# POOL copies the gather's indices itself, the target logits are picked four slots at a time ahead of the waits for rows, and the logits reach the buckets by small matmuls

## The reference

```python
h = (x_flat @ W_gat).reshape(M, HEADS, NUM_EXPERTS)
a_src = (h * att_src).sum(-1)
a_dst = (h * att_dst).sum(-1)
e = leaky_relu(a_src[src] + a_dst[dst], 0.2)
ee = exp(e - segment_max(e, dst)[dst])
alpha = ee / (segment_sum(ee, dst)[dst] + 1e-16)
msg = h[src] * alpha[:, :, None]
agg = segment_sum(msg, dst) + b_gat
scores = layernorm(agg, gamma, beta).mean over heads
# per token: the best 2 of 4 experts, softmax of their scores, gated sum of the experts' outputs
```

## Time and profile before

| what | value |
|---|---|
| median of three runs | 1071.6 us (1069.84 to 1073.52) |
| the profiled execution | 1072.75 us, span 1071.0 us |
| mean granted TensorE clock | 0.869 |
| busy: PE, DVE, ACT, POOL | 793.4, 668.0, 355.3, 180.1 us |
| gathers (L592) | 88 of 1085 ns in the mean, from 825.8 to 975.3 us |

### The profile page before, as it was taken

One profiled execution on the slowest core, in us unless ns is written; L12 is line 12 of the kernel. 1 busy time (PEld: TensorE's weight loads), 2 busy tenths in 40 slices (PEclk: granted clock), 3 DMA queues, 4 the chain that ended last, 5 costly groups with the idle time before them and its releaser, 6 DMA issues.

```text
span 1071.0 us, 15105 instructions
## 1 busy us (share of the span) xinstructions
PE 793.4 (74%) x4837; PEld 519.7 (49%) x4837; DVE 668.0 (62%) x1393; ACT 355.3 (33%) x552; POOL 180.1 (17%) x179
## 2 busy tenths in 40 slices
PE   4369920017999989989988788799759877662688
PEld 1212220016887878878853233444327555442477
DVE  3599778755656656646648777595664434435764
ACT  3421130004544544545542333430022443333451
POOL 5180010000000000000022000100001366773021
PEclk9589965557999999999999899999977988886599
DMA  8000000001000000000000000000012200010001
GB/s 310 0 1 1 1 0 0 2 39 42 2 1 0 0 0 0 0 0 0 0 0 1 0 0 0 2 1 0 2 42 16 8 7 7 7 6 4 3 21 59
DMA packets 15645, 15.63 MB, mean 15 GB/s; under 512 B 9664, under 2 KB 13376, under 8 KB 15216
## 3 DMA queue, kind: packets, MB, share of 16 engines
q1 hardware_dynamic: 12544, 14.00, 4.3%
q0 software_dynamic: 3056, 1.08, 1.7%
HBM read 10.42 MB, written 4.65 MB: 14 GB/s over the span
## 4 chain that ended last, share of the span: by engine, by line
PE 19%; DVE 16%; issue 12%; POOL 3%; DMA 2%; DVEq 2%; ACT 2%; POOLq 0%; PEldq 0%; PEld 0%; SPq 0%; ACTq 0%
PE banks L1557 17%; DVE kept L1229 2%; POOL rows_g L592 2%; DMA rows_g<-table_d,g_idx 2%; DVE wide_buf L1189 1%; DVE wide_buf L1195 1%; PE banks L1838 1%; DVE tie L1193 1%; DVE kept L1292 1%; DVE kept L1386 1%; DVE T L867 1%; DVE round_k L1291 1%; PE banks L1590 1%; DVE shared L1384 1%; ACT wide_buf L776 1%
## 5 line engine op out<-in xcount | busy, mean ns | idle before, releaser
L1138 DVE TENSOR_TENSOR wide_buf<-banks,small 128x1024 f32<-128x1024 f32 x72 | 88.2, 1225 | 117.9 <-ACT small L726 117.9
L1557 PE MATMUL banks<-wide_buf 128*128 128x256 f32 (+1 forms) x720 | 144.6, 349 | 0.0
L1557 PEld LDWEIGHTS banks<-wide_buf 128*128 128x128 f32 x720 | 122.3, 194 | 12.6
L1557 PEld LDWEIGHTS banks<-XP 128*128 128x128 bf16 (+1 forms) x1552 | 101.8, 132 | 47.2 <-DVE XP L992 27.6
L1557 PE MATMUL banks<-XP 128*128 128x32 bf16 (+1 forms) x1552 | 102.4, 213 | 29.5 <-DVE XP L992 27.4
L592 POOL DMA_INDIRECT rows_g<-table_d,g_idx x88 | 95.5, 1085 | 132.2 <-issue 100.4
L1557 PE MATMUL banks<-taps_w,small 128*128 128x128 f32 x618 | 92.2, 296 | 21.0 <-issue 21.0
L1557 PE MATMUL banks<-T,XP 128*128 (+1 forms) x128 | 73.7, 701 | 38.2 <-ACT XP L789 33.3
L1557 PEld LDWEIGHTS banks<-taps_w,small 128*128 128x128 f32 x618 | 85.6, 203 | 31.7 <-issue 22.0
L724 ACT ACTIVATE small<-banks,neg_x 128x512 f32<-128x512 f32 x72 | 49.6, 690 | 150.1 <-PE banks L1557 124.2
L1557 PE MATMUL banks<-shared,sel 128*128 x216 | 60.2, 385 | 32.8 <-DVEq L1131 26.0
(11 more groups left out here) (330 smaller groups left out, 1190.9 us busy)
## 6 DMA issues: line engine op xcount, KB each, us to landing
wide_buf<-in_edges SPq DMA_DIRECT2D x2, 1536.0 KB, 15.4
generic_d<-generic SPq DMA_DIRECT2D x1, 2064.0 KB, 7.3
X<-in_x SPq DMA_DIRECT2D x4, 512.0 KB, 5.3
out_x<-X SPq DMA_DIRECT2D x4, 512.0 KB, 2.6
rows_g<-table_d,g_idx POOLq DMA_INDIRECT x88
wide_buf<-in_edges SPq DMA_DIRECT2D x2, 512.0 KB, 10.0
XP<-in_m_w SPq DMA_DIRECT2D x2, 512.0 KB, 4.7
taps_w<-in_w_dcn SPq DMA_DIRECT2D x1, 576.0 KB, 16.3
```

The source lines that it names most:

```text
L1138: nc.vector.tensor_tensor(near_w[s % RING], banks[:, 0:2, :], hat_x[:, h:h + 1, :].to_broadcast([P, 2, CHUNK]), ALU.mult).then_inc(w_done, 1)
L1557: return nc.tensor.matmul(o, l, r, start=start, stop=stop, **kw)
```

## The change

The indices are no longer copied by DVE: POOL copies four of them in front of each half's gathers and waits for its own copy. DVE's step is two equal halves: first the picks of four slots, then the wait for their rows, then the copy of features and the addition. The target logits no longer pass through DRAM: PE multiplies columns of `a_dst` with slices of the identity (16 matmuls of 128x32 by 128x32), placed in the experts' first iteration, and DVE copies the result. For that a bucket holds another set of 32 nodes: `neg_lo` becomes an input, the layout of `bucket_dst` is head by head, and `slot_sums` takes `q, j = divmod(p, 32)`. `slot_ends` moves ahead of the last node's logits.

```diff
-            sp.wait_ge(adst_ready, 1)
-            sp.dma_start(table_d_dst.rearrange("(t p) h -> p t h", p=P), a_dst[:, :, :]).then_inc(adst_in, 16)
             sp.wait_ge(table_out, 16)
             sp.dma_start(last_row[:, :], table_d[LAST].partition_broadcast(P)).then_inc(last_in, 16)
-            sp.wait_ge(adst_in, 16)
-            sp.dma_start(bucket_dst[:, :, :], table_d_dst.rearrange("(p t) h -> p t h", t=HIS)).then_inc(adst_in, 16)
...
-            def gather(asked, free):
+            def gather(g, r):
                 for half in range(2):
-                    pool.wait_ge(idx1_ready, asked + half + 1)
+                    cols = slice(half * HALF_STEP, (half + 1) * HALF_STEP)
+                    pool.wait_ge(max1_done, g * 2 + half + 1)
                     pool.sem_inc(passed, 1)
-                    pool.wait_ge(max1_done, free + half + 1)
+                    nc.gpsimd.tensor_copy(g_idx[:, cols], slot_idx[:, bass.ds(r * STEP + half * HALF_STEP, HALF_STEP)]).then_inc(idx1_ready, 1)
+                    pool.wait_ge(idx1_ready, g * 2 + half + 1)
                     pool.sem_inc(passed, 1)
...
+                for half in range(2):
+                    cols = bass.ds(r * STEP + half * HALF_STEP, HALF_STEP)
+                    grid = [P, HALF_STEP, HEADS, HIS]
+                    step(nc.vector.tensor_tensor(oh_slots, his[:, cols].unsqueeze(2).to_broadcast([P, HALF_STEP, HIS]),
+                                                 lane[:, 0:HIS].unsqueeze(1).to_broadcast([P, HALF_STEP, HIS]), ALU.is_equal))
+                    step(nc.vector.tensor_tensor(pick_grid, oh_slots.unsqueeze(2).to_broadcast(grid),
+                                                 bucket_dst[:, :, :].unsqueeze(1).to_broadcast(grid), ALU.mult))
+                    step(nc.vector.tensor_reduce(z_by_head[:, :, cols].rearrange("p h k -> p k h"), pick_grid, AX_X, ALU.add))
                     for landed in rows_landed[half]:
                         dve.wait_ge(landed, g * (16 * 2) + 16 * 2)
                         dve.sem_inc(passed, 1)
-                    step(nc.vector.tensor_copy(g_idx[...], slot_idx[...]))
-                    dve.sem_inc(idx1_ready, 1)
-                    step(nc.vector.tensor_copy(feat_s[...], rows_step[...]))
+                    nc.vector.tensor_copy(feat_s[:, :, cols], rows_step[:, half, :, 0:HE].rearrange("p k f -> p f k"))
                     step(nc.vector.tensor_tensor(z_by_head[:, :, cols], z_by_head[:, :, cols], rows_step[...], ALU.add))
                     dve.sem_inc(max1_done, 1)
...
             dve.sem_inc(max1_done, 2)
+            dve.wait_ge(dst_turned, 1)
+            run(nc.vector.tensor_copy(bucket_dst[:, :, :].rearrange("p h t -> p (h t)"), ps[6][:, 0:P]))
+            slot_ends()
             a_src = table[:, :, HE:ROW]
...
-            slot_ends()
-            dve.wait_ge(adst_in, 32)
...
-            with pe.Fori(0, CHUNKS - 1) as i:
+            hidden(0, 0)
+            hidden(0, 1)
+            expert_out(0, 0)
+            pe.wait_ge(adst_ready, 1)
+            for q in range(4):
+                part = slice(q * HIS, (q + 1) * HIS)
+                for h in range(HEADS):
+                    last = mm(ps[6][part, h * HIS:(h + 1) * HIS], a_dst[:, :, h], ident[:, part], True, True)
+            last.then_inc(dst_turned, 1)
+            hidden(0, 2)
+            expert_out(0, 1)
+            hidden(0, 3)
+            expert_out(0, 2)
+            expert_out(0, 3)
+            with pe.Fori(1, CHUNKS - 1) as i:
                 experts(i)
...
                 for p in range(P):
-                    j, q = divmod(p, 4)
+                    q, j = divmod(p, HIS)
```

More of the change, by code:

```diff
@@ L327, in metaformer_kernel @@
         rows_landed = [[rows1_in, sem("rows1_b")], [sem("rows2_in"), sem("rows2_b")]]
-        adst_ready, adst_in, keys_there = (sem(n) for n in ("adst_ready", "adst_in", "keys_there"))
+        adst_ready, dst_turned, keys_there = (sem(n) for n in ("adst_ready", "dst_turned", "keys_there"))
         ends_ready, ends_turned, oh_ready, k_chain, s_chain = (sem(n) for n in (
@@ L466, in _ @@
             pool.dma_start(b_off[0:3 * TAPS, :], a["b_off"].rearrange("(p c) -> p c", c=1)).then_inc(wa_in, 16)
-            for own, name in ((neg_y, "neg_y"), (neg_x, "neg_x"), (y_win, "y_win"), (x_own, "x_own")):
+            for own, name in ((neg_y, "neg_y"), (neg_x, "neg_x"), (neg_lo, "neg_lo"), (y_win, "y_win"), (x_own, "x_own")):
                 pool.dma_start(own[:, :], a[name]).then_inc(wa_in, 16)
@@ L480, in _ @@
                            allow_small_or_imprecise_dtypes=True).then_inc(made2, 1)
-            nc.gpsimd.iota(neg_lo[:, :], [[0, 1]], base=0, channel_multiplier=-(1 << 17),
-                           allow_small_or_imprecise_dtypes=True).then_inc(made2, 1)
+            pool.sem_inc(made2, 1)
             nc.gpsimd.memset(below[:, :, :], 1.0).then_inc(made2, 1)
@@ L593, in gather @@
                                                 bass.IndirectOffsetOnAxis(ap=g_idx[:, c:c + 1], axis=0)).then_inc(rows_landed[half][k // 2], 16)
+            pool.wait_ge(ends_ready, 1)
             with pool.Fori(0, steps) as r:
-                gather(2 * r, 2 * r)
+                gather(r, r)
             with pool.If(rest > 0):
                 with pool.Fori(0, rest) as k:
+                    pool.wait_ge(ends_ready, k + 2)
+                    pool.sem_inc(passed, 1)
                     with pool.Fori(0, STEPS) as r:
-                        gather(k * (2 * STEPS + 2) + (2 * STEPS + 2) + 2 * r, k * (2 * STEPS) + 2 * STEPS + 2 * r)
+                        gather(k * STEPS + STEPS + r, r)
                     pool.nop()
@@ L1325, in _ @@
             norm(ln3, res3, 2)
-            SLOT_KEYS, SLOT_STEP = 13, 3 + 2 * 3
+            SLOT_KEYS, SLOT_STEP = 11, 2 * (3 + 1)
             def slot_keys(R):
@@ L1337, in slot_keys @@
                 step(nc.vector.tensor_tensor(slot_idx[:, 0:P], slot_idx[:, 0:P], slot_lo, ALU.add))
-                for half in range(2):
-                    halves = slice(half * HALF_STEP, (half + 1) * HALF_STEP)
-                    step(nc.vector.tensor_copy(g_idx[:, halves], slot_idx[:, halves]))
-                    dve.sem_inc(idx1_ready, 1)
                 step(nc.vector.tensor_scalar(slot_int, slot_int, 12, None, ALU.arith_shift_right))
@@ L1370, in rows_in @@
                         dve.sem_inc(passed, 1)
-                    step(nc.vector.tensor_copy(g_idx[:, half * HALF_STEP:(half + 1) * HALF_STEP], slot_idx[:, bass.ds(at + STEP, HALF_STEP)]))
-                    dve.sem_inc(idx1_ready, 1)
-                    step(nc.vector.tensor_copy(feat_s[:, :, bass.ds(at, HALF_STEP)], rows_step[:, half, :, 0:HE].rearrange("p k f -> p f k")))
-                def logits_in(half):
-                    cols = bass.ds(r * STEP + half * HALF_STEP, HALF_STEP)
+                    nc.vector.tensor_copy(feat_s[:, :, cols], rows_step[:, half, :, 0:HE].rearrange("p k f -> p f k"))
                     step(nc.vector.tensor_tensor(z_by_head[:, :, cols], z_by_head[:, :, cols],
@@ L1959 @@
               "x_own": f32(np.arange(P)[:, None] % SIDE - 1 + kx), "neg_y": -rows.astype(np.float32),
+              "neg_lo": -f32((np.arange(P) % HIS * 4 + np.arange(P) // HIS)[:, None] * (1 << 17)),
               "neg_x": -(np.arange(P)[:, None] % SIDE).astype(np.float32), "x": np.asarray(inputs["x"])}
```

20 lines of the change are left out of this document (4 added, 16 removed).

## The result

The changed kernel took 1089.5 us (median of 4, 1084.2 to 1099.2) beside 1071.1 of the kernel before: a ratio of 1.0179, 95% interval 1.0103 to 1.0256. It is slower, and outside the range of the forecast. The profiled execution took 1087.37 us, 14.5 more in span than before.

The account below looks back on a forecast made before the run. Two chains side by side, the gathers ending last with only 5.5 us to spare over the experts' loop. 1072.75 - 7.9 - 1.1 + 8.7 = 1072.45 us profiled, 1071.3 on the median's scale, called 1071; 8-in-10 range 1060 to 1083.

Parts of the forecast that it names:

- the pace of the experts' loop: Experts' loop beside gathers keeps 23.95 us an iteration, ending at 974.1; first exponential 7.9 us earlier, not 17.5.
- rival (b): Experts' loop slows as POOL's rest goes: 1079.8 us at 27 us an iteration, 1086 at 30; chance 0.29.
- Rival (a): Experts' loop under gathers runs better than 20 us an iteration, so the gathers set the end: 1061.7 us; chance 0.33.
- The steps: Gather steps: 6.0 us per half, collision included, so ten steps of 12.0 us from 842.3; POOL is the bound.
- The 1.1 us after the first exponential: DVE's product behind the first exponential: its two earlier operations are long done, a gain of 1.1 us.
- the sums: Bucket sums on PE: 256 instructions in one quarter after another at 53.5 ns, 13.7 us against 4.98, +8.7.
- The start: Part before step 1 of the gathers: step 1 begins at 842.3 instead of 850.29, 8.0 us earlier.
- The collision of picks and gathers: Gather steps: two shorter DVE products lie beside gathers in each step, adding 0.15 us per half.
- The 0.69 us a product that I had named as the worst: Gather steps: under an exclusive port lock every product could cost its full 0.69 us, ten steps 10 us longer.
- My +4.5 for a clock that rises halfway: Bucket sums: with PE at 2.4 GHz for the second half, they would cost +4.5 us.
- The 12.8 us: Bucket sums: the skill's some 60 cycles a matmul, at 1.2 GHz, make 12.8 us, +7.8.

Follow-up runs that it names:

- r9: The changed kernel run again without edits on a third chip: 1053.6 us, ratio 0.9847 to the kernel before.
- c15: Changed kernel with bucket sums in the old order, POOL starting a step only when DVE has done both halves of the step before: 1079.3 us (1.0092).
- r10: The kernel before run again without edits on the third chip: 1069.9 us (0.9996).
- c14: Changed kernel with bucket sums in the old order and `bucket_dst` heads innermost, so the picks' multiply is strided: 1057.9 us (0.9870).
- c13: The changed kernel run again without edits on a fourth chip: 1089.0 us, ratio 1.0181 to the kernel before.
- e1: Changed kernel with only the 256 bucket-sum products put back in the old order, round the four column quarters: 1083.0 us (1.0137).

## Why the prediction was wrong

**Failed step: the pace of the experts' loop.** "Kept at that pace", 23.95 us an iteration, was the term; it measured 35.0 in the result and 15.33 in r9. The first put the loop's end at 993.5 where I had 974.1, the second took the loop off the path. The pace was not a constant to be carried over: it depended on how the gathers follow each other, which is what the change alters. I had seen this as rival (b), by the rest on POOL that goes away, which c15 bears out, but stopped its price at 30 us and 1086, and gave it 0.29; the range ended at 1083. The trace of before has a sign of it that I had not put in numbers: seven of its nine held copies start 10.0 to 11.6 us into a step of the gathers, under the stretched eighth gather or in the rest behind it.

**Rival (a), the gathers set the end,** came true in r9, at 1053.6 where I had 1061.7. I had put the holding down to executions being profiled; that is wrong, since the unprofiled runs of the changed kernel took 1084 to 1099 in the one group and 1053 to 1054 in the other. Its sum was off in three terms. The steps: 5.75 us a half (nine steps of r9 take 103.6 us) where I had 6.0, 5 us over 20 halves. The 1.1 us after the first exponential exist only where ACT is late; where the gathers set the end, 14.41 us pass from it to the sums in r9 (959.82 to 974.23), and as many in r10. And the sums.

**The start:** forecast step 1 at 842.3, 8.0 us earlier; 841.62 in the result, and 839.47 against 847.42 in the pair r9 and r10, 7.95. Right. The logits' copy was itself held for 2.1 us in the result (827.71 against 825.56).

**The steps:** POOL's own copy takes 0.20 us, as priced, and the wait behind it 0.79 us, where I had 0.95. The collision of picks and gathers came, but hardly cost anything: POOL's gathers have a mean of 0.96 to 0.97 us with the contiguous multiply. One gather in a step starts under the product, in r9 (timelines of DVE and POOL):
```profile
875.92 0.69 DVE L1366 TENSOR_TENSOR shared<-shared,bucket_dst 128x512 f32<-128x512 f32 x1
...
876.40 1.03 POOL L588 DMA_INDIRECT rows_g<-table_d,g_idx  x1 [0.30 <-issue]
```
It ends 0.82 us behind the product, as the strided pair of c14 above does (0.83), and that of the earlier trace rows (0.82). Only 0.21 us of the short product were left when it started, so it lost 0.08 us. In all traces together, 224 gathers start under such a product so early that their usual 0.94 us would be over less than 0.80 us behind it. Of these 220 end 0.80 to 0.86 us behind it, whether it is strided or not; the other four stand in the last step. A product that starts under a gather keeps its 0.69 us. The Trainium skill (SBUF — State Buffer, section SBUF: two separate sides) calls the shared port pair of DVE and GpSimd an exclusive lock, which a DVE instruction with two SBUF inputs takes only against a GpSimd instruction that reads SBUF. That these gathers behave as if locked out until the product's end agrees with a lock; whether an indirect DMA counts as such a reader, no row tells. The 0.69 us a product that I had named as the worst did not come, since a gather loses only what is left of the product.

**The sums:** 10.61 us, +5.6 instead of +8.7. The price of an instruction was right, and the clock was not: I took the lower one throughout. Stretches of the result's sums, their first third and their last (columns as above), and the whole of c13's:
```profile
1008.49:1012.00 3.51, 3.51 (x69) 3.51 (x70) 1.05 (x1) 0.00 (x0) 0.00 (x0) 0.50 0.00 0
...
1016.00:1019.10 3.10, 3.09 (x101) 2.99 (x98) 0.00 (x0) 0.00 (x0) 0.00 (x0) 1.00 0.02 5
```
```profile
1007.48:1016.89 9.41, 9.41 (x256) 9.31 (x256) 1.05 (x1) 0.00 (x0) 0.00 (x0) 0.81 0.02 3
```
At the granted clock of 0.50 (1.2 GHz) an instruction takes 51 ns, at 1.00 (2.4 GHz) 31 ns. PE works without a gap from 1008.49 on, and the granted clock goes from 0.50 to 1.00 at about 1015; in c13 it rose earlier, and the sums took 9.41 us. My +4.5 for a clock that rises halfway is also a slip: 128 x 53.5 ns and 128 at half of that are 10.3 us, +5.3. The Trainium skill (TensorEngine Tiling (Array Packing), Performance Considerations) has some 60 cycles for each matmul, which is 50 ns at 1.2 GHz; the row at that clock agrees with its 51 ns. The 12.8 us that I made of it would have needed the lower clock to the end.

## What to carry to other kernels

The price of a wait whose sender the profile does not name ("remote") could not be carried over here: ask what makes it come and go, and give both ends a place in the range. A slack of 5 us hid 49 us of such waits in the kernel before, and a change that shortens the one chain uncovers the other; before calling the result, run the same kernel on several chips, since medians of the kernel before that agree to 0.3% said nothing of it. Parts that each gain may lose together, so the parts are worth running alone and in pairs.

## What the runs showed of the hardware

- While POOL issues gathers, ACT can start up to 13.6 us (17.8 in e1, 883.71 to 901.49) after the end of the product of PE that it waits for, in one group of runs and not in another, with the same kernel; ACT's wait is 1.19 to 1.20 us again once the gathers are over. What sets the condition is open: in their first groups two chips showed it in every kernel and two others in none, and one of the first two did not show it in its second group.
- Where it exists, the holds depend on how the gathers follow each other: 35.7 us an iteration in the changed kernel, 18.7 with one gather in four stretched by 0.2 to 0.5 us, 16.1 with 2.3 us more of rest a step; but 23.1 in the kernel before, which rests too.
- A strided second operand makes the same 512-element multiply of DVE 1.10 instead of 0.69 us. A gather of POOL that starts under this multiply and would end sooner ends 0.80 to 0.86 us behind it, strided or contiguous (220 of 224); beside L1350, which reads one operand from PSUM, gathers of the result take 0.94 to 0.97 us as ever.
- 256 matmul instructions of 24 columns take 5.2 us in turn over the four column quarters, at a granted 0.50 throughout, and 9.4 to 10.6 us quarter by quarter, at a mean of 0.81 to 0.69: 51 ns each at 0.50, 31 ns at 1.00.
